# A six-layer decoder kernel: keys turned and copied ahead of the feed-forward work, in halves of one bank, with norms of queries and keys made apart

## The reference

```python
q = l2norm(q) * qs
k = l2norm(k) * ksc
q = q * cos * scale + rotate_half(q) * sin * scale
k = k * cos * inv + rotate_half(k) * sin * inv
...
sim = jnp.einsum('bhwie,bhwje->bhwij', bq, bk2) * QK_SCALE   # window 32, looks back one window
attn = jax.nn.softmax(sim, -1)
out = jnp.einsum('bhwij,bhwje->bhwie', attn, bv2)
...
xn = (x - mu) / jnp.sqrt(var + 1e-05) * g + bln              # feed-forward part
hg = xn @ W1 + b1
a, gate = jnp.split(hg, 2, -1)
return a * jax.nn.gelu(gate, approximate=False) @ W2 + b2
```

## Time and profile before

| | |
|---|---|
| median of 3 runs | 2229.53 us (2228.61 to 2232.08) |
| the profiled execution | 2231.51 us, of which 2229.7 us lie between first and last instruction |
| mean granted clock of PE | 0.983 of full speed |
| PE busy | 2018.6 us (91%) |
| DVE, ACT busy | 1360.2 us, 1361.2 us (61% each) |
| POOL busy | 1079.6 us (48%) |
| DMA, mean | 57 GB/s |
| chain that ended last | PE 64%, ACT 16%, issue 9%, DVE 7%, POOL 4% |

### The profile page before, as it was taken

How to read it: one execution, slowest core, us unless ns; L and a number is a source line. 1 busy time by engine, 2 the same in 40 slices (tenths; PEclk the granted TensorE clock), 3 DMA queues, 4 the chain that set the end, 5 groups by cost and what they waited for, 6 DMA issues and landing times.

```text
span 2229.7 us, 73531 instructions
## 1 busy us (share of the span) xinstructions
PE 2018.6 (91%) x32616; PEld 1196.2 (54%) x32616; DVE 1360.2 (61%) x1663; ACT 1361.2 (61%) x1672; POOL 1079.6 (48%) x708
## 2 busy tenths in 40 slices
PE   7999998688999998999999999999899999999987
PEld 4655655355555555555555555555555555555552
DVE  1444444666666766666667666666666666667662
ACT  5555554355666666656666666666666666666664
POOL 0000000476555555555556555655565555555640
PEclk9999998799999999999999999999999999999998
DMA  3000000122223222232222322222232223222220
GB/s 105 1 1 1 1 20 29 29 68 59 59 59 87 68 68 59 59 87 67 70 59 60 83 62 76 74 55 69 76 77 68 60 57 89 68 68 59 59 59 19
DMA packets 81911, 128.02 MB, mean 57 GB/s; under 512 B 17214, under 2 KB 28092, under 8 KB 81468
## 3 DMA queue, kind: packets, MB, share of 16 engines
q1 hardware_dynamic: 81596, 123.33, 21.3%
HBM read 21.55 MB, written 1.05 MB: 10 GB/s over the span
## 4 chain that ended last, share of the span: by engine, by line
PE 64%; ACT 16%; issue 9%; DVE 7%; POOL 4%; POOLq 0%; SPq 0%; DMA 0%; ACTq 0%; DVEq 0%
PE ps L599 14%; PE ps L625 7%; PE ps L603 7%; PE ps L663 5%; PE ps L680 5%; PE ps L656 5%; PE ps L415 4%; ACT KT L977 4%; PE ps L643 3%; PE ps L608 2%; POOL work L1392 2%; DVE work L1070 2%; PE ps L612 2%; DVE work L1067 2%; ACT ps L968 2%
## 5 line engine op out<-in xcount | busy, mean ns | idle before, releaser
L1392 POOL TENSOR_TENSOR work<-work,RS 128x1024 f32<-128x1024 f32 x192 | 361.6, 1904 | 309.9 <-ACT RS L1011 309.9
L603 PEld LDWEIGHTS ps<-ident,work 128*128 128x128 f32 x3072 | 343.6, 142 | 150.5 <-issue 73.5
L1067 DVE TENSOR_TENSOR work<-ps,work 128x1024 f32<-128x1024 f32 x192 | 230.9, 1203 | 311.6 <-ACT work L990 301.3
L603 PE MATMUL ps<-ident,work 128*128 128x128 f32 x3072 | 392.9, 276 | 28.1 <-ACT work L964 12.0
L1386 POOL TENSOR_TENSOR work<-work 128x1024 f32<-128x1024 f32 x96 | 226.2, 2357 | 371.3 <-DVE work L1070 371.3
L599 PE MATMUL ps<-WK,XS 128*128 128x512 f32 x384 | 188.8, 614 | 50.9 <-ACT KT L977 50.8
L1070 DVE TENSOR_TENSOR work<-ps,work 128x1024 f32<-128x1024 f32 x192 | 233.2, 1215 | 0.0
L1106 DVE TENSOR_REDUCE SS<-work 128x16 f32<-128x1024 f32 x192 | 232.1, 1209 | 0.0
L1379 POOL TENSOR_TENSOR work<-work 128x1024 f32<-128x1024 f32 x96 | 226.3, 2357 | 4.3 <-DVE work L1070 4.3
L937 ACT ACTIVATE work<-ps 128x1024 f32<-128x1024 f32 x96 | 98.1, 1022 | 209.2 <-PE ps L663 207.3
L663 PEld LDWEIGHTS ps<-work 64*32 64x32 f32 x12288 | 135.8, 106 | 163.2 <-issue 106.4
(11 more groups left out here) (183 smaller groups left out, 3071.3 us busy)
## 6 DMA issues: line engine op xcount, KB each, us to landing
work<-work SPq DMA_DIRECT2D x576, 128.0 KB
work<-work SPq DMA_DIRECT2D x336, 64.0 KB
WQ<-in_wqkv SPq DMA_DIRECT2D x6, 512.0 KB, 3.7
WK<-in_wqkv SPq DMA_DIRECT2D x6, 512.0 KB, 4.4
WV<-in_wqkv SPq DMA_DIRECT2D x6, 512.0 KB, 3.7
WO<-in_wo SPq DMA_DIRECT2D x6, 512.0 KB, 3.8
work<-ZR SPq DMA_DIRECT2D x48, 64.0 KB
W<-in_w SPq DMA_DIRECT2D x6, 341.0 KB, 2.9
```

The source lines that it names most:

```text
L603: m = nc.tensor.transpose(flat(R)[:, t * 128:t * 128 + 128], src[:, t * 128:t * 128 + 128], ident[:, :])
L1067: V.tensor_tensor(h16(cos_part[:, j, :]), h16(flat(src)), rotary_tabs[:, at:at + 64].unsqueeze(1).broadcast_to([PARTS, 16, 64]), ALU.mult) ...
L1392: U.tensor_tensor(h16(qk_norm[:, j, :]), h16(cos_part[:, j, :]), inv_norms[:, j, :].unsqueeze(2).broadcast_to([PARTS, 16, 64]), ALU.mult). ...
```

## The change

The edits, by engine:

- **PE**: the heads are turned before the values are projected; the keys are turned before the FFN work instead of behind it, and signalled after each half (4 of 8 transposes); the projection of the keys waits and signals by half. In step 1 the hidden chunks are regrouped: `hid(1)` whole ahead of the first weigh, the gate of chunk 2 between the weighs, its value behind them.
- **ACT**: the heads are copied before the values; keys are copied and squared in two halves of 512 columns; Ln and Exp of the norms are made twice, once for the queries (16 columns, before the keys' squares) and once for the keys at the step's end, now ahead of the copy of the heads in steps 0, 2 and 3. In step 1 the copy of the heads moves behind the third gelu and stays ahead of the table load. The first table load moves behind the copy of the keys, ahead of the copy of the queries. The last FFN norm operation leaves ACT.
- **DVE**: the keys are rotated in halves; there is a clamp behind each of the sums; the FFN norm is two operations here; the second gating moves behind the maximum and its subtraction.
- **POOL**: the queries' product comes ahead of the keys' rotation, so that only the keys' product is left behind it.

The core of the diff:

```diff
@@ tensor, step @@
                     project(bank_z, w_q, 1, n).then_inc(q_projected, 1)
+                if d:
+                    pe.wait_ge(heads_copied, g - 2)
+                    turn(bank_y, heads).then_inc(heads_turned, 1)
                 if b:
...
                     m.then_inc(values_ready, 1)
-                if d:
-                    pe.wait_ge(heads_copied, g - 2)
-                    turn(bank_y, heads).then_inc(heads_turned, 1)
+                if b:
+                    pe.wait_ge(k_normed, g)
+                    if d:
+                        pe.wait_ge(heads_turned_copied, g - 2)
+                    turn(bank_y, qk_norm[:, 1, :], 0, 4).then_inc(k_turned, 1)
+                    turn(bank_y, qk_norm[:, 1, :], 4, 8).then_inc(k_turned, 1)
...
                 if a:
                     pe.wait_ge(wk_loaded, 16 * (g // 16 + 1))
-                    if due(g):
-                        pe.wait_ge(k_turned_copied, g)
-                    project(bank_y, w_k, 0, n)
-                    project(bank_y, w_k, 1, n).then_inc(k_projected, 1)
+                    for half in range(2):
+                        if due(g):
+                            pe.wait_ge(k_turned_copied, 2 * g - 1 + half)
+                        project(bank_y, w_k, half, n).then_inc(k_projected, 1)
...
                     pe.wait_ge(hidden_gated, 3 * f + 1)
-                    hid_gate(1, bank_f)
+                    hid(1, bank_f)
...
-                    hid_value(1, bank_f)
+                    pe.wait_ge(gate_gelu, 3 * f + 2)
+                    hid_gate(2, bank_f)
...
                     pe.wait_ge(hidden_gated, 3 * f + 2)
-                    hid(2, bank_f)
+                    hid_value(2, bank_f)
@@ scalar @@
+            def invert_norms(g, j):
+                act.wait_ge(sums_clamped, 2 * g + 1 + j)
+                A(norm_logs[:, 16 * j:16 * j + 16], sq_clamped[:, 16 * j:16 * j + 16], ACT.Ln).then_inc(norms_log, 1)
...
+                A(inv_norms[:, j, :], norm_logs[:, 16 * j:16 * j + 16], ACT.Exp, scale=-0.5).then_inc(inverse_norms, 1)
...
+                if b:
+                    for half in range(2):
+                        act.wait_ge(k_turned, 2 * g - 1 + half)
...
+                        A(k_t[:, 4 * half:4 * half + 4, 32 + 128 * par:160 + 128 * par], bank_y[:, half, :].rearrange('p (c t) -> p c t', t=128), ACT.Copy).then_inc(k_turned_copied, 1)
+                if f is not None and n == 1:
+                    if a:
+                        invert_norms(g, 0)
+                    nc.scalar.preload_act_table_set(GELU)
...
-                if c:
-                    copy_heads(g)
                 if f is not None and n == 1:
                     gelu(f, 2, bank_f)
+                    copy_heads(g)
                     nc.scalar.preload_act_table_set(LNEXP)
...
+                    if a:
+                        invert_norms(g, 1)
+                else:
+                    if a:
+                        invert_norms(g, 1)
+                    if c:
+                        copy_heads(g)
@@ vector, step @@
-                    rotary(g, n, 1, bank_y, k_cos, k_sin, k_rotated)
+                    for half in range(2):
+                        dve.wait_ge(k_squared, 2 * g + 1 + half)
...
+                        rotary_cos(g, n, 1, bank_y[:, half, :], slice(512 * half, 512 * half + 512), k_cos)
...
+                        rotary_sin(g, n, 1, bank_y[:, half, :], slice(512 * half, 512 * half + 512), k_sin)
```

More of the change, by code:

```diff
@@ L599, in project, with turn @@
                 return mm(R[:, half, :], x_shift[:, 32 + at * 128:160 + at * 128], w[:, half * 512:half * 512 + 512], start=True, stop=True)
-            def turn(R, src):
-                for t in range(8):
+            def turn(R, src, first=0, last=8):
+                for t in range(first, last):
                     m = nc.tensor.transpose(flat(R)[:, t * 128:t * 128 + 128], src[:, t * 128:t * 128 + 128], ident[:, :])
@@ L945, in step @@
                     A(probs[:, :, :, :], scores_sb[:, :, :, :], ACT.Exp).then_inc(probs_exp, 1)
-                if f is not None and n == 1:
-                    ffn_affine(f)
                 if a:
@@ L965, in step @@
                 if b:
+                    act.wait_ge(values_ready, g)
+                    if due(g - 1):
+                        act.wait_ge(windows_loaded, 160 * (g - 1))
+                    A(v_rows[:, (n - 1) % 2, :], flat(bank_x), ACT.Copy).then_inc(values_copied, 1)
+                if b:
                     act.wait_ge(values_copied, g)
@@ L971, in step @@
                 if f is not None and n == 1:
-                    nc.scalar.preload_act_table_set(GELU)
-                if b:
-                    act.wait_ge(k_turned, g)
-                    if due(g - 1):
-                        act.wait_ge(scores_ready, g - 1)
-                    A(k_t[:, :, 32 + 128 * par:160 + 128 * par], turned(bank_y), ACT.Copy).then_inc(k_turned_copied, 1)
-                    act.wait_ge(q_turned, g)
-                    A(q_t[:, :, :], turned(bank_z), ACT.Copy).then_inc(q_turned_copied, 1)
-                    if n == 2:
-                        act.wait_ge(k_turned_copied, g)
-                        A(k_t[:, :, 0:32], k_t[:, :, 256:288], ACT.Copy).then_inc(keys_carried, 1)
-                if f is not None and n == 1:
                     gelu(f, 0, bank_f)
+                elif a:
+                    invert_norms(g, 0)
                 if a:
-                    act.wait_ge(k_projected, g + 1)
-                    if due(g):
-                        act.wait_ge(k_sums, g)
-                    A(squares[:, 1, :], flat(bank_y), ACT.Square).then_inc(k_squared, 1)
+                    for half in range(2):
+                        act.wait_ge(k_projected, 2 * g + 1 + half)
+                        if due(g):
+                            act.wait_ge(k_sums, g)
+                        A(squares[:, 1, 512 * half:512 * half + 512], bank_y[:, half, :], ACT.Square).then_inc(k_squared, 1)
                 if c:
@@ L1102, in sums @@
             def sums(j, squared, done, g):
-                dve.wait_ge(squared, g + 1)
+                dve.wait_ge(squared, (j + 1) * (g + 1))
                 if due(g):
-                    dve.wait_ge(sums_clamped, g)
+                    dve.wait_ge(sums_clamped, 2 * g - 1 + j)
                 V.tensor_reduce(sq_sums[:, j, :], h16(squares[:, j, :]), AX, ALU.add).then_inc(done, 1)
+                dve.wait_ge(done, g + 1)
+                if due(g):
+                    dve.wait_ge(norms_log, 2 * g - 1 + j)
+                V.tensor_scalar(sq_clamped[:, 16 * j:16 * j + 16], sq_sums[:, j, :], 1e-24, None, ALU.max).then_inc(sums_clamped, 1)
             def step(g, n, a, b, c, d, f, fo):
@@ L1129, in step @@
                 if a:
-                    dve.wait_ge(k_squared, g + 1)
-                    if due(g):
-                        dve.wait_ge(k_normed, g)
-                    rotary(g, n, 1, bank_y, k_cos, k_sin, k_rotated)
-                if f is not None and n == 1:
-                    gated(f, 1, bank_f)
+                    for half in range(2):
+                        dve.wait_ge(k_squared, 2 * g + 1 + half)
+                        if due(g):
+                            dve.wait_ge(k_normed, g)
+                        rotary_cos(g, n, 1, bank_y[:, half, :], slice(512 * half, 512 * half + 512), k_cos)
+                        if due(g):
+                            dve.wait_ge(k_rotated, g)
+                        rotary_sin(g, n, 1, bank_y[:, half, :], slice(512 * half, 512 * half + 512), k_sin)
                 if b:
```

88 lines of the change are left out of this document (42 added, 46 removed).

## The result

The changed kernel takes 2272.26 us (median of 4 runs, 2262.98 to 2277.94), the kernel before on the same chip 2230.81 us: a ratio of 1.0183, 95% interval 1.0152 to 1.0214. The forecast of 2219 us was wrong in sign and the time lies outside its range of 2188 to 2246.

What follows compares the result with a forecast made beforehand. PE's own work plus its waits bound the kernel. Steps sum to -0.15 us a pass, times 22 -3.5; with 7 saved outside, -10.5 from 2231.5 gives 2221, the median 2.0 lower: 2219 us, range 2188 to 2246.

Steps and rivals of the forecast that it cites:

- The waits at the keys' projection, steps 0 and 3: PE starts the keys' projection at 7.7 instead of 8.17 in step 0; step 3 loses its 0.33 us wait.
- Step 0: First step of a pass: gain 0.7 us, from 16.26 to 15.55, with the keys' projection starting earlier.
- step 3: Last step of a pass: gain 0.65 us, to 16.75, from a wait of 0.33 and slow start of 0.17 going.
- its wait before the weigh: Step 0, PE waiting 0.91 us for the keys' rotation: stays nearly whole, because new norms stand in ACT's way.
- The halves: Keys' rotation on DVE split into 512-column halves: 0.61 us each, so four take 2.44 us instead of 2.26.
- Rival A: Halves on DVE and ACT don't overlap and cost whole rows: 0.85 us more a pass, 2238 us; chance 0.20.
- Step 2: Loss of 1.7 us, from 18.34 to 20.0: new PE wait of 1.8 at the keys' turn for the copied turned heads.
- Step 1: Gain 0.5 us, from 20.55 to 20.05; queries' clamp done at 8.7, scores starting at 11.65.
- my 0.85: PE's wait in us at step 1's first scores, released by the queries' copy, replacing 1.32 at the keys' projection.
- a term that I had at 0.5: FFN norm's move from ACT: DVE 0.5 us more, ACT 0.8 less, beside a PE that waits for neither.
- Rival D: PE's clock falls each time behind step 2's wait of 1.8: 3 us or more a pass, 2290 us; chance 0.03.
- The 7 us outside the passes: Blocks 1 to 7 and 96 on: one POOL product before the turn instead of two; half of 13 us gained.

Runs made afterwards that it cites:

- the first experiment: Changed kernel with both clamps written as a reduction (maximum over pairs of the sum and a stored 1e-24) in place of tensor_scalar: 2235.66 us, ratio 1.0038.
- The repairs: Two separate single edits to the changed kernel: heads' copy ahead of the third gelu, 2250.88 us; step 2's keys' turn behind the second feed-forward matrix, 2233.87 us.
- the best version: Changed kernel, clamps as reductions, heads' copy before third gelu, step 2's keys' turn behind second feed-forward matrix, step 1's queries' norms late: 2168.52 us (2162.00, half the transfers delayed).

## Why the prediction was wrong

**The waits at the keys' projection, steps 0 and 3: right in kind, short in size.** Those waits went. Step 0 gained 0.59 of 0.7, step 3 0.34 of 0.65. The stops account for part of what is missing: 0.38 a pass in step 3 where they were 0.19, and 1.02 in step 0 where they were 0.51. That step 0 comes near its forecast is partly luck. I kept its wait before the weigh "nearly whole" at 0.91; all its waits together fell from 1.41 to 0.44, 0.97 and not 0.7, and the stops took half of that back.

**The halves: right.** A half takes 0.60 from start to start (1174.58 to 1175.18), its row is 0.68; I took 0.61. Rival A is out. The 0.66 that I worked out from the Trainium skill ("VectorE: DVE Perf Modes", section on the TRN2 errata) lies near the row of 0.68 and not near the distance, and it is the distance that the sum needs.

**Step 2: right.** The wait is 1.82 where I had 1.8, with the releaser that I named, and an undisturbed step takes 19.80 where I had 20.0. Its mean is 20.42, by stops of 0.46 a pass and the one fall of the clock. The repairs show that this wait was a price of the order, not of the idea.

**Step 1: here the prediction failed, in one term.** I wrote "DVE needs 3.64 to the queries' sums, 1.3 for them and 0.18 for the clamp: 8.7". The sums were in fact done earlier; the clamp started at 8.07 and ended at 9.47, since it takes 1.40. With 0.17 it would have ended at 8.24, hardly behind the keys' copy on ACT (7.94), and the wait would have been the 0.92 of the first experiment. The price came from one row, a clamp behind the keys' sums, at which POOL happened to rest. The trace before had one sign of it: of its 96 clamps 95 take 0.18 us, and one, the very first, 1.33, ending 0.04 behind a POOL operation. Nothing in my sum asked what POOL does at that moment; the queries' clamp stands right behind the queries' rotation, and the end of that rotation is just what starts POOL's addition of 2.36. The order of the program gave this away: a clamp that comes one sum of 1.21 behind the rotation must meet an addition of 2.36. That the first experiment's 0.92 lies so near my 0.85 is partly luck too: without the long clamp the scores start at 11.19 (1144.87 to 1156.06) where I had 11.65, and PE begins the keys' projection at 8.35 where I had about 9.0, because the keys' clamp of step 0 was done 0.20 into step 1 and not 1.1. Both ends were half a microsecond early. The same blocking met a term that I had at 0.5, the FFN norm's last operation on DVE: it takes 0.49 where POOL rests and 2.05 at the median of its 24 places.

**The clock: the right mechanism at the wrong place.** Rival D had 0.03, and looked only at step 2's wait of 1.8, which indeed left the clock alone. The wait that I had priced at 0.85 became 2.1, and behind it the clock fell in 9 of 21 passes. So the mis-sized 1.2 us cost 1.17 a pass as a wait (2.09 less 0.92) and up to 0.9 as clock.

**Outside the passes and the stops.** The 7 us outside the passes were half of a bound; what came was a loss of 1.4 (and -0.15 times 22 is -3.3, not -3.5). By ratio the forecast missed by 2.3%, 51 us: 32 are the clamp with its clock, 8 lie outside the passes. The stops were in the earlier trace rows's own view, in other steps of it, and I read only waits that another engine ends. They went up by 1.12 a pass, 25 us. With the reduction in place they are 1.51 a pass above the kernel before, more than the 0.37 by which the pass is then longer, so they are enough to hide what the change gained elsewhere (1.0038). What makes them grow when PE's waits move is not settled: a third goes with the transfers. That PE's earlier waits gave the list time to arrive would fit packets that never start less than 3.2 us apart, and is not shown.

## What to carry to other kernels

Before an operation's price is taken from a row, look at what the other engines do in the row and at the new place: a 16-column operation that is moved beside a GpSimd operation can take as long as that one, and another form of the same operation may be free of it. Follow the chain behind it to the first engine that waits, and then ask whether that wait grows to a size behind which this kernel has lost clock: here waits of 1.8 us in step 2 left the clock alone, and waits of 2.1 in step 1 cost 0.75 to 1.2 us a pass of it on top of themselves. When all waits are accounted for, read the stops without a releaser too; with fewer waits they were the largest idle time left in the best version.

## What was new about the hardware

- A VectorE `tensor_scalar` of 128 x 16 took 0.17 us alone and 1.40 beside a GpSimd addition in SBUF (1.75 at most in the changed kernel), and ended 0.03 us behind the GpSimd operation each time; a `tensor_reduce` of twice as many inputs took 0.186 in every one of 192 places.
- The granted clock fell to its lower level behind TensorE waits of 2.1 to 2.5 us in 9 to 15 of 21 passes, never behind waits of 1.82 us at one place in three kernels, and also behind single stops of 1.5 to 2.0 us that no engine made.
- TensorE stopped for up to 1.7 us at fixed instructions of the program, 0.95 us a pass before and 2.07 after. Every such stop ended 1.2 to 1.6 us behind the landing of a 16.4 KB packet of its own instructions. With an eighth of the largest transfers two thirds of the changed kernel's stops were left.
